# A graph layer's last stage: the sum of each row and its normed row made on GpSimd instead of ScalarE

## The chip, the cores and the metric

The kernel runs on one core of a Trainium2 chip. The metric is the device time of one execution in microseconds: the median over repeated runs of the kernel, without the profiler. The profile is of one further execution.

## The reference

A graph of 12,500 nodes with 256 channels and 212,500 weighted edges goes through one layer of four parts, all in float32:

```
xn = layernorm(x)
x  = x + segment_sum(w * (xn @ W)[dst], src) + mix(xn)   # linear attention, a small MLP, two layer norms
xh = layernorm(x)
s  = xh @ wr + br                      # one score for each row
sel = the 6249 rows with the highest scores
y  = (gelu(xh[sel] @ w1 + b1) @ w2 + b2) * s[sel]
out = x + xh;  out[sel] += y
```

What matters here is the last part. Every row needs its normed row `xh`, since the selected ones go through the feed-forward network, and the sum `x + xh`, which is the output of the rows that are not selected and the base to which the others add.

## The kernel before, in words

**Rows and tiles.** The 12,500 rows lie in 98 tiles of 128 rows. After the graph part and the mixing part, `x` of all rows stands in SBUF as `acc`, 98 tiles side by side, 256 float32 to a tile. The last stage handles them in 14 groups of G = 7 tiles; a group has 7 x 256 = 1792 columns.

**Up to the stage.** A loop sums sorted edge messages: VectorE builds weighted one-hots (L1822), TensorE multiplies, ScalarE evicts, and GpSimd adds 128x256 blocks into `acc` (L728). Then VectorE takes the statistics of every tile and the products with `wr` (L1841, L1843), ScalarE sums the products into the scores (L1348), and VectorE works out `rstd` and `minus` = -mean * rstd (L1861). Line 1862 makes `twice` = rstd + 1. The semaphore `norm_set` tells ScalarE that they are there.

**ScalarE's pass, `tail_rows` (L1352).** For a group n it writes, tile by tile, the normed rows `acc * rstd + minus` into one half of `rowbuf` (L1357, seven activations of 128x256), then the scores into a 257th column (L1359), and then, tile by tile, `acc * twice + minus` = x + xh into `x3[s]` (L1363, seven more). `rowbuf` has two halves and `x3` two buffers, `node` and a part of `tabs`; before a group writes one, it waits until the store of the group two before it has landed (`x3_out`, `base_out`). Each activation adds 1 to `rows_ready`, so 15 come from a group.

**SyncE's stores, `tail_store` (L594).** It waits for 8 of a group's 15 and stores the half of `rowbuf` to `sorted_rows` in HBM (L596, 903 KB), then waits for all 15 and stores `x3[s]` to the output (L605, 896 KB). All is in the order of the groups on one queue.

**VectorE meanwhile: the top-k.** From L1870 on it searches the score that 6249 rows reach, two bits a round in 16 rounds (L1881 to L1897). A round is a chain of small operations, each waiting for the one before: it forms three candidates (L1885, L1877 to L1879), compares the 98 scores of each partition with each (L1888, three times 128x98), counts (L1891), has TensorE sum the counts over the partitions (L1089), reads them from PSUM (L1894), and takes the bits over (L1895, L1897). Afterwards two prefix sums give each row its place (L1911 to L1918), and VectorE writes large one-hots over parts of `acc` that are no longer needed (L1949 to L1952, after the wait at L1948 for eight groups' `rows_ready`), then seven times L1957; TensorE turns them into the list of selected rows (L1105), and L1963 hands the first numbers to GpSimd.

**GpSimd meanwhile** has nothing to do: after L728 its next instruction is the first gather of selected rows, `x_fetch` (L741), which waits for the last stores and for `xid_ready` from L1963. From there to the end the feed-forward network runs over 25 blocks of 256 selected rows on TensorE (L1116 to L1135), with ScalarE, VectorE and GpSimd beside it.

Of the kernel before, what the change touches and what calls it, by code (L numbers as in the profile page):

```python
# [6 lines left out]
N, C, E, HEADS, HID, NQKV = 12500, 256, 212500, 8, 1024, 768  # L7
P = 128
# [35 lines left out]
G = 7  # L44
NG = NT // G
# [5 lines left out]
def gps_layer_kernel(nc, x, src, dst, edge_weight, gnn_w, wqkv, ln1_g, ln1_b, w1, b1, w2, b2,  # L51
# [3 lines left out]
    ALU, ACT, AX = mybir.AluOpType, mybir.ActivationFunctionType, mybir.AxisListType  # L55
    ds = bass.ds
# [14 lines left out]
    with ExitStack() as ctx:  # L71
        def sb(name, shape, dt=F32):
            return ctx.enter_context(nc.sbuf_tensor(name, shape, dt))

        def sem(name):
            return ctx.enter_context(nc.semaphore(name))


        acc = sb("acc", [P, NT * C])
# [22 lines left out]
        rowbuf = sb("rowbuf", [P, 2 * S, RW])  # L102
# [34 lines left out]
        def part(at, *shape, of=acc):  # L137
            n = int(np.prod(shape))
            ap = of[:, at:at + n]
            if len(shape) == 1:  # L140
                return ap
            if len(shape) == 2:
                return ap.rearrange("p (a b) -> p a b", a=shape[0])
            return ap.rearrange("p (a b c) -> p a b c", a=shape[0], b=shape[1])

        def half(at, n, of, dt=BF16):
            return of[:, at:at + n // 2].bitcast(dt)
# [6 lines left out]
        fw1_s = tabs[:, 0:CC * HID].rearrange("p (c h) -> p c h", c=CC)  # L154
        fw2_s = tabs[:, CC * HID:2 * CC * HID].rearrange("p (k c) -> p k c", c=C)
# [12 lines left out]
        GC = G * C  # L168
# [63 lines left out]
        wts, idx, place, rstd = (part(2560 + k * NT, NT, of=mb) for k in range(4))  # L232
# [6 lines left out]
        minus, twice, tile_b = part(4500, NT, of=mb), part(4600, NT, of=mb), half(4700, NT, mb)  # L239
# [9 lines left out]
        x3 = [node[:, 0:GC], tabs[:, 2 * CC * HID:2 * CC * HID + GC]]  # L249
# [50 lines left out]
        (qT_in, xnb_in, x_in, t_mm, x1_ready, x1T_mm, x1T_ready, h_mm, h_ready, y_mm, mix_done) = (sem(n) for n in (  # L300
            "qT_in", "xnb_in", "x_in", "t_mm", "x1_ready", "x1T_mm", "x1T_ready", "h_mm", "h_ready", "y_mm",
            "mix_done"))
        fw_in, w_in, w2_in, t_read, xnb_read, xb_ready, y_left = (sem(n) for n in (
            "fw_in", "w_in", "w2_in", "t_read", "xnb_read", "xb_ready", "y_left"))
        rows_left, norm_ready = sem("rows_left"), sem("norm_ready")
        passed, bits_ready = sem("passed"), sem("bits_ready")
        r_in = [sem(f"rows_in{k}") for k in range(KB)]
# [9 lines left out]
        base_out = [sem(f"base_out{s}") for s in range(2)]  # L317
# [63 lines left out]
        def _(sp):  # L381
# [205 lines left out]

            sp.wait_ge(perm_mm, NSB)
            sp.wait_ge(rhs_ready, NSB)
            sp.dma_start(fw1_s, fw1.rearrange("(k p) c -> p k c", p=P)).then_inc(fw_in, 16)  # L590
            sp.dma_start(fw2_s, fw2.rearrange("(k p) c -> p k c", p=P)).then_inc(fw_in, 16)


            def tail_store(g, s, last=False):  # L594
                sp.wait_ge(rows_ready, (2 * G + 1) * g + G + 1)
                sp.dma_start(lanes(tiles_of(rows_d[0:NT * P, :])[ds(G * g, G)]), rowbuf[:, s * G:(s + 1) * G, :]).then_inc(  # L596
                    x3_out[s], 16)
                sp.wait_ge(rows_ready, (2 * G + 1) * (g + 1))
                rows_ = x3[s].rearrange("p (t c) -> p t c", t=G)
                if last:  # L600
                    sp.dma_start(lanes(tiles_of(out[(NT - G) * P:(NT - 1) * P, :])), rows_[:, 0:G - 1, :]).then_inc(
                        base_out[s], 16)
                    sp.dma_start(out[(NT - 1) * P:N, :], rows_[0:LASTROWS, G - 1, :]).then_inc(base_out[s], 16)
                else:
                    sp.dma_start(lanes(tiles_of(out[0:(NT - 1) * P, :])[ds(G * g, G)]), rows_).then_inc(base_out[s], 16)  # L605

            with sp.Fori(0, NG // 2 - 1) as i:
                for s in range(2):
                    tail_store(2 * i + s, s)
            tail_store(NG - 2, 0)  # L610
            tail_store(NG - 1, 1, last=True)


        @block.gpsimd
        def _(pool):
            g = nc.gpsimd
# [19 lines left out]
            with pool.Fori(0, NG // 2) as i:  # L636
                chain.enter(i, 2 * G * 2)
                for n in range(2 * G):
                    s, t = n // G, n % G
# [90 lines left out]


            pool.sem_inc(fo_free, FO0)

            def x_fetch(i, s, after=True):

                pool.wait_ge(xid_ready, i + 1)
                if after:
                    pool.wait_ge(x3T_mm, i - 1)
                pool.sem_inc(passed, 1)
                for u in range(2):  # L740
                    g.indirect_dma_start(xc[s][:, u, :], None, rows_d[0:NT * P, :],  # L741
                                         bass.IndirectOffsetOnAxis(xid[:, s, u:u + 1], 0)).then_inc(xc_in[s], 16)
# [37 lines left out]
        def _(pe):  # L780
# [22 lines left out]
            for k, tab in enumerate((fbkt, floc, rew, fdrel)):  # L803
# [4 lines left out]
                for q in range(4):  # L808
                    n = min(4, T - 4 * q)
# [263 lines left out]
            with pe.Fori(0, steps) as i:  # L1073
                for k in range(KB):
                    pe.wait_ge(r_in[k], 16 * (i + 1))
                    pe.wait_ge(sums_ready, KB * i + k + 1)
                    for h in range(2):
                        grp = RG * i + 2 * k + h
                        for t in range(2):
                            pe.wait_ge(ohw_ready, 2 * grp + t + 1)  # L1080
                            s = 2 * h + t
# [19 lines left out]
            for q in range(G):  # L1101
                pe.wait_ge(cnt_ready, 18 + 3 + q)
                for t in range(LT):
                    i = LT * q + t
# [1 line left out]
                              start=i == 0, stop=i == NT - 1)  # L1106
                last.then_inc(cnt_mm, 1)

            pe.wait_ge(fw_in, 32)

            def served_transpose(i, s, turn):
                pe.wait_ge(xc_in[s], 32 * (turn + 1))
# [44 lines left out]
        def _(act):  # L1157
            A = nc.scalar.activation
# [13 lines left out]
            for job, o in enumerate(wq):  # L1172
                act.wait_ge(tab_mm, job + 1)
                if job == 4:
                    act.wait_ge(wraw_in, 112)
                    for c in range(CC):
                        last = A(o[:, c * C:(c + 1) * C], ps[:, job % 8, c * C:(c + 1) * C], ACT.Copy,
                                 scale=g1_c[:, c:c + 1])
# [5 lines left out]
            for k, outs in enumerate(tables):  # L1184
                for q in range(4):
                    job, n = 6 + 4 * k + q, min(4, T - 4 * q)
# [165 lines left out]
            def tail_rows(n, s, first=False):  # L1352

                if not first:
                    act.wait_ge(x3_out[s], 8 * (n - s))
                for t in range(G):
                    A(rowbuf[:, s * G + t, 0:C], acc[:, ds(n * GC + t * C, C)], ACT.Identity,  # L1357
                      scale=rstd[:, ds(G * n + t, 1)], bias=minus[:, ds(G * n + t, 1)]).then_inc(rows_ready, 1)
                A(rowbuf[:, s * G:(s + 1) * G, C], wts[:, ds(G * n, G)], ACT.Copy).then_inc(rows_ready, 1)  # L1359
                if not first:  # L1360
                    act.wait_ge(base_out[s], 8 * (n - s))
                for t in range(G):
                    A(x3[s][:, t * C:(t + 1) * C], acc[:, ds(n * GC + t * C, C)], ACT.Identity,  # L1363
                      scale=twice[:, ds(G * n + t, 1)], bias=minus[:, ds(G * n + t, 1)]).then_inc(rows_ready, 1)

            act.wait_ge(norm_set, 3)
            for s in range(2):
                tail_rows(s, s, first=True)
            with act.Fori(1, NG // 2) as i:
                for s in range(2):  # L1370
                    tail_rows(2 * i + s, s)
# [17 lines left out]
        def _(dve):  # L1389
            v = nc.vector  # L1390
# [222 lines left out]
            for q in range(4):  # L1613
                n = min(4, T - 4 * q)
# [221 lines left out]
            with dve.Fori(0, NG // 2) as i:  # L1836
                chain.enter(i, 2 * (2 * G + 1))
                for s in range(2):
                    n = 2 * i + s
# [19 lines left out]
            v_link(v.tensor_scalar(wts[:, :], wts[:, :], br_c[:, 0:1], None, ALU.add))  # L1859

            v.scalar_tensor_tensor(minus, mv[:, :, 0], -1.0, rstd[:, :], ALU.mult, ALU.mult).then_inc(norm_set, 1)  # L1861
            v.tensor_scalar(twice, rstd[:, :], 1.0, None, ALU.add).then_inc(norm_set, 1)
            v.sem_inc(norm_set, 1)
            chain.inc(v.tensor_copy(tile_b, cols[:, 0:NT]))
            chain.inc(v.memset(idl[:, 2 * FP:2 * FP + 4], 0))
# [79 lines left out]
            v_link(v.tensor_scalar(rI, pI, P - 1, None, ALU.bitwise_and))  # L1945
            chain.inc(v.tensor_copy(dv, dI))
            v_link(v.tensor_copy(md, rI))
            dve.wait_ge(rows_ready, (2 * G + 1) * 8)  # L1948
            v_link(v.tensor_tensor(spots, dv.unsqueeze(1).to_broadcast([P, 2 * FP, NT]),  # L1949
                                   cols[:, 0:2 * FP].unsqueeze(2).to_broadcast([P, 2 * FP, NT]), ALU.is_equal))  # L1950
            v.tensor_scalar(marks[:, 0, :, :], spots, lane[:, 0:1], None, ALU.mult).then_inc(cnt_ready, 1)
# [97 lines left out]
```

## Time and profile before

| | |
|---|---|
| median of 3 runs | 3774.55 us (3771.11 to 3775.57) |
| the profiled execution's own time | 3799.59 us |
| its span, first to last instruction | 3797.8 us |
| busy: TensorE matmul, VectorE, GpSimd, ScalarE | 3073.4, 2599.6, 2113.8, 1555.3 us |
| last stage before the feed-forward network | about 3296 to 3409 us of the span |
| feed-forward network | about 3415 us to the end |

The profile is one execution, with start and duration of every instruction on each engine, the semaphores that released it, and every DMA packet. PE is TensorE, PEld its weight loads, DVE VectorE, ACT ScalarE, POOL GpSimd, SPq the queue of SyncE on which the DMAs are issued. A duration is the time from the start of an instruction to its end, and holds whatever the instruction waited for in between.

### The profile page before, as it was taken

The numbers are of one execution on the slowest core, as the hardware profiler recorded it, in microseconds if no ns is written. First come the engines' busy times: TensorE is split into PE (matmuls) and PEld (weight loads), VectorE is DVE, ScalarE is ACT, GpSimd is POOL, SyncE is SP. The second block draws the span as 40 slices with busy tenths as digits, with TensorE's granted clock in tenths as the row PEclk, the third lists the DMA queues.
The fourth block names the chain that finished last, engine by engine and source line by source line (L and its number), as shares of the span: only waits on it lengthen the run. The fifth ranks groups of instructions, "written<-read, shape, count | busy, mean of one in ns | idle before, by whom it ended". The sixth has DMA issues, their size and how long they took to land.

```text
span 3797.8 us, 81728 instructions
## 1 busy us (share of the span) xinstructions
PE 3073.4 (81%) x18820; PEld 2305.1 (61%) x18820; DVE 2599.6 (68%) x6591; ACT 1555.3 (41%) x3781; POOL 2113.8 (56%) x2304
## 2 busy tenths in 40 slices
PE   3777738888888788888888886999999997029998
PEld 2444426666666666666676664777777775018887
DVE  6888884444444677777787773999999999861111
ACT  4444404555555444444444443333333333673222
POOL 1445534555555566666666565777777776003433
PEclk7899969999999999999899898999999999559999
DMA  5777727787777766666677666888888887161111
GB/s 162 239 262 261 256 73 239 263 261 254 252 264 262 237 229 217 216 215 222 222 228 231 203 211 221 272 278 276 277 276 277 277 277 229 62 217 50 54 52 44
DMA packets 427482, 818.33 MB, mean 215 GB/s; under 512 B 45499, under 2 KB 203191, under 8 KB 427256
## 3 DMA queue, kind: packets, MB, share of 16 engines
q1 hardware_dynamic: 348376, 559.80, 48.5%
q0 software_dynamic: 78880, 256.49, 17.7%
q14 instruction: 203, 1.66, 0.1%
q8 instruction: 23, 0.38, 0.0%
HBM read 459.96 MB, written 356.17 MB: 215 GB/s over the span
## 4 chain that ended last, share of the span: by engine, by line
PE 38%; issue 14%; DVE 14%; POOL 13%; ACT 6%; another core or an unknown queue 6%; DMA 3%; POOLq 3%; SPq 1%; DVEq 1%; ACTq 0%
POOL acc L728 13%; PE ps L948 12%; PE ps L1135 5%; PE ps L1125 5%; PE ps L961 3%; PE ps L995 2%; ACT rowbuf L1261 2%; POOLq L725 2%; PE ps L1082 2%; PE ps L1004 2%; DVE acc L1490 2%; PE ps L957 1%; DMA rowbuf<-sorted_rows 1%; DMA acc<-bucket_rows 1%
## 5 line engine op out<-in xcount | busy, mean ns | idle before, releaser
L695 POOL DMA_INDIRECT sorted_rows<-rowbuf,posu x896 | 1003.4, 1120 | 768.2 <-ACT rowbuf L1261 554.3
L948 PE MATMUL ps<-mainbuf 128*128 128x256 bf16 x5376 | 731.5, 280 | 195.7 <-ACT rowbuf L1261 140.5
L1082 PE MATMUL ps<-rowbuf,mainbuf 128*128 128x256 f32 x3584 | 844.7, 392 | 25.9 <-DVE mainbuf L1822 20.9
L1822 DVE TENSOR_SCALAR mainbuf<-cols,rowbuf 128x128 f32<-128x128 f32 x1792 | 820.9, 528 | 58.5 <-DMA rowbuf<-sorted_rows 50.2
L728 POOL TENSOR_TENSOR acc<-acc,node 128x256 f32 x896 | 673.3, 751 | 196.3 <-POOL acc L728 156.1
L1082 PEld LDWEIGHTS ps<-rowbuf,mainbuf 128*128 128x128 f32 x3584 | 620.3, 189 | 250.1 <-DVE mainbuf L1822 177.5
L948 PEld LDWEIGHTS ps<-mainbuf 128*128 128x128 bf16 x5376 | 502.2, 100 | 338.8 <-ACT rowbuf L1261 187.7
L1261 ACT ACTIVATE rowbuf<-ps 128x512 f32<-128x512 f32 x896 | 515.4, 594 | 447.2 <-PE ps L948 371.5
L1341 ACT ACTIVATE node<-ps 128x512 f32<-128x512 f32 x448 | 267.6, 597 | 603.0 <-PE ps L1082 499.4
L1665 DVE TENSOR_SCALAR mainbuf<-mainbuf,lane 128x1024 bf16<-128x1024 bf16 (+1 forms) x256 | 117.4, 458 | 254.4 <-PE ps L948 194.7
L1648 DVE TENSOR_TENSOR mainbuf<-tabs,cols 128x1664 bf16<-128x1664 f32 (+1 forms) x128 | 241.1, 1884 | 0.0
L1658 DVE TENSOR_REDUCE wl<-ps 128x14 f32<-128x28 f32 x128 | 24.1, 188 | 278.4 <-remote 245.0
L1331 ACT ACTIVATE rowbuf<-ps,fb_c 128x256 f32<-128x256 f32 x200 | 94.9, 474 | 253.7 <-PE ps L1125 245.2
L741 POOL DMA_INDIRECT acc<-sorted_rows,posu x50 | 48.6, 973 | 265.7 <-DVE posu L1963 197.3
L1252 ACT ACTIVATE wl<-ps 128x14 f32<-128x14 f32 x128 | 24.4, 190 | 407.8 <-DVE wl L1659 333.4
L961 PE MATMUL ps<-wqkvT,acc 128*128 128x512 f32 x392 | 185.5, 596 | 0.0
L852 PE MATMUL ps<-acc,mainbuf 128*128 128x416 f16 x512 | 125.4, 376 | 73.8 <-DVE acc L1490 73.8
L1135 PE MATMUL ps<-tabs,rowbuf 128*128 128x256 f32 x800 | 179.2, 382 | 5.4 <-ACT rowbuf L1331 5.1
L1125 PE MATMUL ps<-acc,tabs 128*128 128x256 f32 x800 | 179.3, 383 | 0.8 <-ACT acc L1326 0.8
L1135 PEld LDWEIGHTS ps<-tabs,rowbuf 128*128 128x128 f32 x800 | 149.9, 190 | 30.7 <-issue 9.6
L1651 DVE TENSOR_TENSOR mainbuf<-mainbuf,tabs 128x1092 bf16<-128x1092 bf16 x128 | 164.9, 1288 | 0.0
L1125 PEld LDWEIGHTS ps<-acc,tabs 128*128 128x128 f32 x800 | 146.0, 191 | 30.1 <-ACT acc L1326 1.2
(338 smaller groups left out, 4641.1 us busy)
## 6 DMA issues: line engine op xcount, KB each, us to landing
rowbuf<-sorted_rows SPq DMA_DIRECT2D x448, 516.0 KB, 4.5
mainbuf<-slot_rows_in_window SPq DMA_DIRECT2D x128, 448.0 KB
acc<-bucket_rows SPq DMA_DIRECT2D x128, 416.0 KB, 6.1
sorted_rows<-node SPq DMA_DIRECT2D x105, 258.0 KB, 2.4
mainbuf<-support_rows SPq DMA_DIRECT2D x128, 192.0 KB
sorted_rows<-rowbuf,posu POOLq DMA_INDIRECT x896
node<-in_x SPq DMA_DIRECT2D x104, 128.0 KB, 5.1
sorted_rows<-rowbuf SPq DMA_DIRECT2D x14, 903.0 KB, 4.9
```

The source lines that it names most:

```text
L695: g.indirect_dma_start(pairs_d, bass.IndirectOffsetOnAxis(posu[:, PC * k + c:PC * k + c + 1], 0), rowbuf[:, S * k + 2 * c:S * k + 2 * c + ...
L728: g.tensor_tensor(acc[:, ds(at, C)], acc[:, ds(at, C)], sums[:, k, h * C:(h + 1) * C], ALU.add).then_inc(acc_done, 1)
L948: last = mm(ps[:, MSG + (k + c) % 2, u * C:(u + 1) * C], oht[:, s * P:(s + 1) * P], win[:, k, v * C:(v + 1) * C], start=v == 0, stop=v == 2)
L961: last = mm(ps[:, KVPS + u, :], xnT_b[u][:, c * P:(c + 1) * P], wqkvT[:, c, C:3 * C], start=c == 0, stop=c == CC - 1)
L1082: last = mm(ps[:, GRP + k, h * C:(h + 1) * C], ohw[:, k % 2, s * P:(s + 1) * P], rowbuf[:, BT * k + s, 0:C], start=t == 0, stop=t == 1)
L1125: last = mm(ps[:, 2 + m % 2, 0:C], fw1_s[:, c, m * P:(m + 1) * P], x3T[:, s, c * 2 * P:(c + 1) * 2 * P], start=c == 0, stop=c == CC - 1)
L1135: last = mm(ps[:, 4 + s, u * C:(u + 1) * C], fhT[:, s, m, u * P:(u + 1) * P], fw2_s[:, m, :], start=m == 0, stop=m == HID // P - 1)
L1261: A(rowbuf[:, S * k + 2 * c:S * k + 2 * c + 2, 0:C], ps[:, MSG + (k + c) % 2, :].rearrange("p (t c) -> p t c", t=2), ACT.Copy).then_inc(ro ...
L1341: A(sums[:, k, :], ps[:, GRP + k, :], ACT.Copy).then_inc(sums_ready, 1)
L1648: v.tensor_tensor(ohp, pA[:, :, ds(i, 1)].to_broadcast([P, T, P]), cols[:, :].unsqueeze(1).to_broadcast([P, T, P]), ALU.is_equal).then_inc ...
L1651: v.tensor_tensor(rhs, ohs.unsqueeze(3).to_broadcast([P, T, S, V]), metab[:, ds(i, 1), :, :].rearrange("p a t v -> p (a t) v").unsqueeze(2 ...
L1822: v.tensor_scalar(ohw[:, k % 2, s * P:(s + 1) * P], cols[:, :], rowbuf[:, r, C + 1:C + 2], rowbuf[:, r, C:C + 1], ALU.is_equal, ALU.mult). ...
```

## The change

ScalarE writes only the normed rows and the scores: 8 increments of `rows_ready` from a group instead of 15. A new loop on GpSimd, `base_rows`, adds the seven normed tiles in `rowbuf` to the seven tiles of `acc` with one instruction of 128x1792 float32 and writes `x3[s]`; it waits for the group's 8 increments and, from the third group on, for the landing of the output store that last used `x3[s]`. Its semaphore `base_made` releases the output store, and ScalarE waits for it before it writes a half of `rowbuf` again. `twice` is gone. VectorE's wait before L1949 is now for eight `base_made`. To free a semaphore the loads of `fw1` and `fw2` count on `w_in` instead of `fw_in`; TensorE waits for the sum of both at the same place.

```diff
 sync:
-            sp.dma_start(fw1_s, fw1.rearrange("(k p) c -> p k c", p=P)).then_inc(fw_in, 16)
-            sp.dma_start(fw2_s, fw2.rearrange("(k p) c -> p k c", p=P)).then_inc(fw_in, 16)
+            sp.dma_start(fw1_s, fw1.rearrange("(k p) c -> p k c", p=P)).then_inc(w_in, 16)
+            sp.dma_start(fw2_s, fw2.rearrange("(k p) c -> p k c", p=P)).then_inc(w_in, 16)
             def tail_store(g, s, last=False):
-                sp.wait_ge(rows_ready, (2 * G + 1) * g + G + 1)
+                sp.wait_ge(rows_ready, (G + 1) * (g + 1))
...
-                sp.wait_ge(rows_ready, (2 * G + 1) * (g + 1))
+                sp.wait_ge(base_made, g + 1)
 gpsimd, between the loop of L728 and x_fetch:
+            def base_rows(n, s, first=False):
+                pool.wait_ge(rows_ready, (G + 1) * (n + 1))
+                if not first:
+                    pool.wait_ge(base_out[s], 8 * (n - s))
+                pool.sem_inc(passed, 1)
+                g.tensor_tensor(x3[s].rearrange("p (t c) -> p t c", t=G), rowbuf[:, s * G:(s + 1) * G, 0:C],
+                                acc[:, ds(n * GC, GC)].rearrange("p (t c) -> p t c", t=G),
+                                ALU.add).then_inc(base_made, 1)
+
+            for s in range(2):
+                base_rows(s, s, first=True)
+            with pool.Fori(1, NG // 2) as i:
+                for s in range(2):
+                    base_rows(2 * i + s, s)
 tensor:
-            pe.wait_ge(fw_in, 32)
+            pe.wait_ge(w_in, 16 * 6 + 32)
 scalar, tail_rows:
                 if not first:
                     act.wait_ge(x3_out[s], 8 * (n - s))
+                    act.wait_ge(base_made, n - 1)
...
-                if not first:
-                    act.wait_ge(base_out[s], 8 * (n - s))
-                for t in range(G):
-                    A(x3[s][:, t * C:(t + 1) * C], acc[:, ds(n * GC + t * C, C)], ACT.Identity,
-                      scale=twice[:, ds(G * n + t, 1)], bias=minus[:, ds(G * n + t, 1)]).then_inc(rows_ready, 1)
-            act.wait_ge(norm_set, 3)
+            act.wait_ge(norm_set, 2)
 vector:
-            v.tensor_scalar(twice, rstd[:, :], 1.0, None, ALU.add).then_inc(norm_set, 1)
...
-            dve.wait_ge(rows_ready, (2 * G + 1) * 8)
+            dve.wait_ge(base_made, 8)
```

On GpSimd, before, the end of the summing loop is followed at once by the gathers of `x_fetch` (`posu` is where the numbers of the selected rows lie):

```order
L728 TENSOR_TENSOR acc<-acc,node 128x256
L721 REGISTER_ALU
L721 COMPARE_AND_BRANCH
L741 DMA acc<-sorted_rows,posu 128x258 [waits base_out1,xid_ready,x3_out1,x3_out0,base_out0]
L741 DMA acc<-sorted_rows,posu 128x258
```

With the change, the adds of the 14 groups stand between them (lines after 733 are shifted by 15 or less in the changed file; its L756 is the gather):

```order
L728 TENSOR_TENSOR acc<-acc,node 128x256
L721 REGISTER_ALU
L721 COMPARE_AND_BRANCH
L739 TENSOR_TENSOR node<-rowbuf,acc 128x1792 [waits rows_ready]
L739 TENSOR_TENSOR tabs<-rowbuf,acc 128x1792 [waits rows_ready]
L745 UNCONDITIONAL_BRANCH
L745 ISA
L737 REGISTER_ALU [waits rows_ready]
L739 ISA [waits base_out0]
L739 TENSOR_TENSOR node<-rowbuf,acc 128x1792
```

Two stand ahead of a loop of six turns with two each. They were not there before; the gathers behind them are the same.

On SyncE, one turn of the store loop for the even group, before:

```order
L596 ISA [waits rows_ready]
L596 DMA sorted_rows<-rowbuf 128x7x258
L598 ISA
L605 ISA [waits rows_ready]
L605 DMA out_rows<-node 128x7x256
```

and with the change:

```order
L596 ISA [waits rows_ready]
L596 DMA sorted_rows<-rowbuf 128x7x258
L605 ISA [waits base_made]
L605 DMA out_rows<-node 128x7x256
```

The output store, and with it every store behind it on the queue, now waits for GpSimd instead of ScalarE.

## Rows read from the trace of the kernel before

**Rows 1.** The page's part 1: busy time, share of the span, instructions.
```profile
PE 3073.4 (81%) x18820; PEld 2305.1 (61%) x18820; DVE 2599.6 (68%) x6591; ACT 1555.3 (41%) x3781; POOL 2113.8 (56%) x2304
```

**Rows 2.** The chain that ended last, 3250 to 3800 us: start, us, what.
```profile
3390.75 3.44 ACT tabs L1363 x7
3394.18 21.82 issue
3416.08 0.61 ACT acc L1326
```

**Rows 3.** The waits, 3290 to 3430 us: us in total, times, longest.
```profile
POOL acc L741 <- DVE posu L1963: 197.3, 1, 197.3
```

**Rows 4.** Timeline, end of the stretch: start us, us, engine, line, op.
```profile
3378.03 5.26 DVE L1949 TENSOR_TENSOR acc<-mainbuf,cols 128x4900 bf16<-128x4900 f32 x1
...
3389.44 17.80 PE L1105 MATMUL ps<-acc,mainbuf 128*128 128x100 bf16 x98 [18.04 <-DVE mainbuf L1957]
...
3407.76 0.24 DVE L1963 COPY posu<-mainbuf 128x2 uint32<-128x2 uint32 x2
...
3408.96 0.98 POOL L741 DMA_INDIRECT acc<-sorted_rows,posu  x1 [197.34 <-DVE posu L1963]
```

**Rows 5.** Windows: length; busy PE, PEld, DVE, ACT, POOL; clock, DMA share, GB/s.
```profile
3301.30:3303.30 2.00, 0.00 (x0) 0.00 (x0) 0.95 (x7) 2.00 (x5) 0.00 (x0) 0.50 1.00 349
3304.90:3306.90 2.00, 0.00 (x0) 0.00 (x0) 0.97 (x6) 2.00 (x6) 0.00 (x0) 0.50 1.02 346
3300.00:3398.00 98.00, 12.33 (x69) 8.00 (x70) 69.92 (x266) 94.19 (x203) 0.00 (x0) 0.50 0.77 263
3398.60:3408.00 9.40, 8.64 (x48) 5.81 (x46) 5.33 (x8) 0.00 (x0) 0.00 (x0) 0.50 0.01 2
```

**Rows 6.** Timeline, start of the stretch, VectorE and ScalarE.
```profile
3296.19 0.20 DVE L1862 TENSOR_SCALAR mainbuf<-mainbuf 128x98 f32<-128x98 f32 x1
3296.31 0.20 DVE L1864 CAST mainbuf<-cols 128x98 bf16<-128x98 f32 x1
3296.43 3.55 ACT L1357 ACTIVATE rowbuf<-acc,mainbuf 128x256 f32<-128x256 f32 x7 [5.51 <-DVE mainbuf L1862]
...
3299.88 0.20 ACT L1359 ACTIVATE rowbuf<-mainbuf 128x7 f32<-128x7 f32 x1
3299.98 3.53 ACT L1363 ACTIVATE node<-acc,mainbuf 128x256 f32<-128x256 f32 x7
...
3303.42 3.53 ACT L1357 ACTIVATE rowbuf<-acc,mainbuf 128x256 f32<-128x256 f32 x7
```

**Rows 7.** DMA issues, 3290 to 3430 us: count, KB each, us to landing.
```profile
sorted_rows<-rowbuf SPq DMA_DIRECT2D x14, 903.0 KB, 4.9
out_rows<-node SPq DMA_DIRECT2D x7, 896.0 KB, 4.1
```

**Rows 8.** GpSimd's adds by line: count, ns min/median/max, first and last start.
```profile
L644 POOL TENSOR_TENSOR node<-node,rowbuf x49: 662/672/1017, 77.5 to 454.1; 128x256 f32<-128x256 f32 x49
...
L728 POOL TENSOR_TENSOR acc<-acc,node x896: 722/754/847, 2354.1 to 3210.9; 128x256 f32 x180
...
L705 POOL TENSOR_TENSOR node<-node,vec x49: 1268/1277/1289, 1293.8 to 2264.2; 128x512 f32<-128x512 f32 x49
```

**Rows 9.** Timeline around a long GpSimd operation, 499 to 507 us.
```profile
499.00 7.29 POOL L655 TENSOR_TENSOR tabs<-acc,tabs 128x1664 bf16<-128x1664 f32 x1
499.12 1.21 DVE L1468 TENSOR_TENSOR_SCAN mainbuf<-one,ps 128x512 f32<-128x512 f32 x1
...
500.36 5.47 DVE L1474 SCALAR_TENSOR_TENSOR small<-mainbuf 128x4 int32<-128x4 f32 x1
505.87 0.45 DVE L1475 TENSOR_SCALAR small<-small 128x4 int32<-128x4 int32 x1
```

**Rows 10.** VectorE operations by line: count, ns min/median/max.
```profile
L1490 DVE TENSOR_TENSOR acc<-acc,mainbuf x128: 1009/1019/7581, 73.3 to 528.5; 128x1664 f16<-128x1664 f16 x128
...
L1474 DVE SCALAR_TENSOR_TENSOR small<-mainbuf x32: 165/166/5470, 62.1 to 523.9; 128x4 int32<-128x4 f32 x32
...
L1822 DVE TENSOR_SCALAR mainbuf<-cols,rowbuf x1792: 332/346/907, 2348.9 to 3206.5; 128x128 f32<-128x128 f32 x200
...
L1508 DVE BATCH_NORM_STATS2 stats<-node x49: 401/408/428, 63.7 to 409.7; 128x6 f32<-128x256 f32 x49
```

**Rows 11.** Timeline, one of the sixteen top-k rounds.
```profile
3298.29 0.16 DVE L1885 TENSOR_TENSOR cands<-tk,mainbuf 128x3 int32<-128x3 int32 x1 [0.81 <-DVE tk L1874]
...
3299.09 0.63 DVE L1888 TENSOR_SCALAR mainbuf<-mainbuf,cands 128x98 f32<-128x98 f32 x3
3299.76 0.46 DVE L1891 TENSOR_REDUCE cntb<-mainbuf 128x3 bf16<-128x294 f32 x1
...
3300.50 0.16 DVE L1894 TENSOR_SCALAR cands<-ps 128x3 int32<-128x3 f32 x1 [0.28 <-PE ps L1089]
...
3301.01 0.55 DVE L1897 TENSOR_TENSOR tk<-tk,cands 128x1 int32<-128x1 int32 x3
3302.43 0.16 DVE L1885 TENSOR_TENSOR cands<-tk,mainbuf 128x3 int32<-128x3 int32 x1 [0.88 <-DVE tk L1897]
```

More of the change, by code:

```diff
@@ L302, in gps_layer_kernel @@
             "mix_done"))
-        fw_in, w_in, w2_in, t_read, xnb_read, xb_ready, y_left = (sem(n) for n in (
-            "fw_in", "w_in", "w2_in", "t_read", "xnb_read", "xb_ready", "y_left"))
+        base_made, w_in, w2_in, t_read, xnb_read, xb_ready, y_left = (sem(n) for n in (
+            "base_made", "w_in", "w2_in", "t_read", "xnb_read", "xb_ready", "y_left"))
         rows_left, norm_ready = sem("rows_left"), sem("norm_ready")
```

## The prediction

> **What bounds the kernel now.** Part 1 of the page [rows 1] gives TensorE the largest share of the span, but the change lies in one stretch of about 110 us in which TensorE is nearly idle, so the shares say nothing; that stretch has to be read alone. The chain of waits comes next [rows 2]. It names ScalarE's second pass L1363 as the last piece before the feed-forward network, and then 21.82 us of "issue", a stretch that nothing explains. So the chain is not to be trusted there: it fell back on ScalarE's own previous work. The wait list [rows 3] and the end of the timeline [rows 4] say what GpSimd's first gather L741, with which the network begins, waited for: it starts at 3408.96, 0.96 us after VectorE's L1963 is done, and L1963 hangs on TensorE's L1105 (done at 3407.2) and on VectorE's one-hots from L1949 on. The stores, which L741 needs as well, were ready long before: from 3398.6 to 3408.0 the DMA engines are busy for a share of 0.01 [rows 5]. **The bound of the stretch is VectorE's top-k chain**, 3296.3 to 3408.0; ScalarE's two passes and the stores end some 10 us earlier, beside it.
>
> **What is removed.** ScalarE loses 98 activations. By the timeline [rows 6] the first seven L1363 run from 3299.98 until the next group starts at 3303.42, so 3.44 us of each group and 14 x 3.44 = 48 us of ScalarE. All of it lies beside the top-k, with 10 us to spare: worth nothing. If that cover were gone, because VectorE were faster, the stores would bind next. On VectorE L1862 goes: the next instruction starts 0.12 us after it [rows 6], so -0.1 us on the path. The `fw` loads wait for the same things and are waited for at the same place: nothing.
>
> **How fast the new pipeline turns.** A group moves 903 + 896 KB [rows 7], which is 1.84 MB. In the two bursts of [rows 5] the DMA engines have a share of 1.00 and move 346 to 349 GB/s, so a group can't take less than 1.84 MB / 349 = 5.3 us. ScalarE needs 3.5 us for it [rows 6], and GpSimd some 4 us (below). ScalarE waits for the landing of the store two groups before; that takes 4.9 us alone, and more behind another store. So the stores pace the group, at 5.3 us: the last of 14 adds begins at about 3300 + 13 x 5.3 = 3369, and the last store has landed by about 3380. That is earlier than now and still not what L741 waits for.
>
> **What GpSimd's adds cost.** The trace has float32 adds of 256 columns with a median of 672 or 754 ns, and of 512 with 1277 ns [rows 8]. The second 256 columns cost 523 to 605 ns, so 1792 columns are 754 + 6 x 523 = 3.9 us or 672 + 6 x 605 = 4.3 us. I take 4.0 us. The bound above is seven times 754, 5.3 us, as if nothing were saved by one instruction. GpSimd is idle there today [rows 3], so none of this costs anything by itself: 14 x 4.0 = 56 us beside VectorE.
>
> **What the adds do to VectorE.** This is the term that decides. At 499.00 GpSimd begins a 7.29 us operation (L655), which ends at 506.29 [rows 9]. VectorE's L1474, on four columns, starts at 500.36 and takes 5.47 us; by its own row its minimum and median are 165 and 166 ns [rows 10]. L1475 behind it ends at 506.32, when GpSimd is through. The operations on SBUF operands behave alike over the trace: L1490, with two inputs, has a median of 1019 ns and a maximum of 7581; L1822, one input with factors from SBUF, has a minimum of 332 and a maximum of 907 ns in the loop in which L728 (754 ns) runs beside it. Other forms are not held up: L1468, with an input in PSUM, runs from 499.12 to 500.33 under the same L655, and the statistics L1508, with one input, stay between 401 and 428 ns. So a VectorE operation of the first kinds, issued during a GpSimd add, ends when the add ends. The Trainium skill says the same as a rule, in "SBUF — State Buffer", section "Who interferes with whom": the port pair that the two engines share is locked for a whole instruction, and a VectorE instruction with two SBUF inputs, or in a mode that uses both ports, "fully blocks" against GpSimd. By that rule the trace agrees, and a sum that leaves it out would be 46 us too short.
>
> Now one round of the top-k [rows 11]. It takes 4.14 us (3298.29 to 3302.43). L1885 to L1888 and L1895 to L1897 work on SBUF alone and are of the kinds that stop. From L1891 (one input, a reduction) over TensorE's sum to L1894 (from PSUM), 3299.76 to 3300.66, and in the gap of 0.88 us at the end of a round VectorE has nothing of the kinds that stop: 0.90 and 0.88 us in which an add costs nothing. So of an add of 4.0 us VectorE loses all but what it can still do before the next operation that stops: at most one such piece, say 0.9 us up to 1.05 with the waits at its ends, and at least nothing. The fixed part of the held-up instruction is also saved: L1475 took 0.45 us and ended 0.03 us after the add, where an operation of that size takes 0.17 (L1474), so 0.15 us. Recovered are 0.15 to 1.2 us of each add. I take the middle, 0.68, since an add starts where a store has landed, at any point of a round. **VectorE loses 14 x (4.0 - 0.68) = 46.5 us.** Ends: 14 x (3.9 - 1.2) = 38 us and 14 x (5.3 - 0.15) = 72 us.
>
> All 14 adds fall into the top-k: they end by 3373, and VectorE, held up, is then at about its seventh round of sixteen. So L1949's new wait for eight adds (the eighth is done by about 3341) is over long before VectorE comes there, and L1949 and L1957 meet no add. What follows L1949 is only moved: with it L741, and the network behind it.
>
> **Sum:** -0.1 + 46.5 = +46.4 us. Against its own execution: 3799.59 + 46.4 = 3846 us with the profiler. The median of the runs lies 25.0 us under the profiled execution; I take this for the same: 3774.55 + 46.4 = **3821 us**.
>
> **Rivals.**
> *Not slower: the two engines don't get into each other's way here.* The held-up instructions of [rows 9, 10] met GpSimd operations on other tiles; if what stopped them were an access to the same tile's memory, or if the adds with three plain float32 operands were free of it, VectorE would lose nothing, and 3774.4 us would result. Against it: L1822 reads `cols` and `rowbuf` and writes `mainbuf`, while L728 works on `acc` and `node`, as plain as the new add. It is no gain either, since the stores that end sooner aren't waited for. It decides below 0.5 us lost per add: 14 x 0.5 = 7 us, about what a measurement of this kernel can tell from no change (0.2%, 7.5 us). Chance 0.07; and 0.02 that something is faster for a reason I don't see, such as fewer wake-ups on the queues.
> *The add is far slower than the row of adds says.* At 5.3 us (seven single ones, or the address pattern of 7 pieces with a gap of 2 columns in `rowbuf`) it paces the pipeline instead of the DMA engines, above about 5.1 us with the 0.17 us between two. VectorE then gets nearly nothing between two adds: 14 x (5.3 - 0.68) = +65 us, 3839 us. L705 with 512 columns speaks against it. Chance 0.12.
> *Less is lost than I think, 20 to 38 us*, because the adds fall into the free pieces of a round by habit (VectorE runs free for a moment after each), or since only the read or only the write part of an add is exclusive: 3795 to 3812 us, say 3805. L1474 in [rows 9] ended 0.46 us before the add did, which speaks a little for it. Chance 0.14.
>
> **How the numbers follow.** Forecast, 38 to 55 us lost: 0.65. Range 3804 to 3842: it takes in the slow add (3839) and most of the third rival, and leaves out the 0.09 without a loss and the ends beyond. Slower 0.91, same 0.07, faster 0.02.
>
> **What would show it.** In the changed profile: GpSimd's new line with 14 instructions of 4.0 us; L1885 to L1897's counterparts with maxima of about 4 us and unchanged minima, while the reduction stays at 0.46 us; the top-k of 82 us long grown to about 128; ScalarE idle between groups, a period of 5.3 us on GpSimd and SyncE; GpSimd's first gather at 3408.96 + 46 = 3455, still released by VectorE; the network after it of the same length. Wrong would be: maxima of VectorE at their old values, or a first gather released by a store.

## The result, and the profile after

The changed kernel takes **3816.57 us** (median of 4 runs, 3807.39 to 3821.74) against 3772.98 us for the kernel before (4 runs): 43.6 us more, a ratio of 1.0109 with a 95% interval of 1.009 to 1.0129. Forecast were 3821 us, in a range of 3804 to 3842.

The two profiled executions can't be compared by their spans: that of before reached the stretch at 3296.43, that of after at 3266.69, though the work ahead of it is the same, and the profiled execution of before (3799.59 us) was 26.6 us above its median while that of after (3816.30 us) is at it. It is before's execution that is out of line: e2 and e7 below, built on the kernel before, reached the stretch at 3261.34 and 3265.32. So the comparison is made inside the stretch: from ScalarE's first normed row to GpSimd's first gather. Before that was 3296.43 to 3408.96, 112.53 us [rows 4, 6]. After, the timeline of the changed kernel shows (start us, us, engine, line, op):

```profile
3266.69 3.54 ACT L1373 ACTIVATE rowbuf<-acc,mainbuf 128x256 f32<-128x256 f32 x7 [5.39 <-DVE mainbuf L1872]
...
3394.76 5.26 DVE L1959 TENSOR_TENSOR acc<-mainbuf,cols 128x4900 bf16<-128x4900 f32 x1
...
3424.50 0.24 DVE L1973 COPY posu<-mainbuf 128x2 uint32<-128x2 uint32 x2
...
3425.69 0.97 POOL L756 DMA_INDIRECT acc<-sorted_rows,posu  x1 [81.19 <-DVE posu L1973]
```

That is 159.00 us, **46.5 us more**. From the start of L1959 (L1949 before) to the gather it is 30.93 us in both traces, and from the gather to the end 388.8 us in both. So all of it lies in VectorE's top-k, before L1959. The gather is still released by VectorE. GpSimd's new line, by its instructions (ns min/median/max):

```profile
L739 POOL TENSOR_TENSOR node<-rowbuf,acc x7: 3704/3711/3722, 3270.5 to 3335.5; 128x1792 f32<-128x1792 f32 x7
L739 POOL TENSOR_TENSOR tabs<-rowbuf,acc x7: 3616/3620/3647, 3274.2 to 3340.9; 128x1792 f32<-128x1792 f32 x7
```

and VectorE's operations in the sixteen rounds, the counterparts of L1877, L1879, L1888, L1891, L1894 and L1897:

```profile
L1887 DVE TENSOR_SCALAR cands<-cands x16: 168/169/3632, 3268.7 to 3376.6; 128x3 int32<-128x3 int32 x16
...
L1889 DVE TENSOR_TENSOR cands<-cands x16: 164/164/3597, 3269.2 to 3377.0; 128x3 int32<-128x3 int32 x16
...
L1898 DVE TENSOR_SCALAR mainbuf<-mainbuf,cands x48: 257/266/3673, 3269.3 to 3377.6; 128x98 f32<-128x98 f32 x48
...
L1901 DVE TENSOR_REDUCE cntb<-mainbuf x16: 461/461/462, 3270.0 to 3377.9; 128x3 bf16<-128x294 f32 x16
...
L1904 DVE TENSOR_SCALAR cands<-ps x16: 160/160/161, 3270.8 to 3378.6; 128x3 int32<-128x3 f32 x16
...
L1907 DVE TENSOR_TENSOR tk<-tk,cands x48: 158/159/3661, 3274.3 to 3379.5; 128x1 int32<-128x1 int32 x48
```

The minima and medians are those of before; a few instructions of every kind that works on SBUF alone took as long as an add. The operation that reads PSUM never did, though two of its sixteen began while an add ran. The reduction never did either, but here none began during an add, so this trace alone doesn't show that it would pass. The timeline of the changed kernel shows two adds and what they hit:

```profile
3292.13 0.16 DVE L1905 TENSOR_TENSOR cands<-cands,mainbuf 128x3 int32<-128x3 int32 x1
3292.18 3.70 POOL L739 TENSOR_TENSOR node<-rowbuf,acc 128x1792 f32<-128x1792 f32 x1 [2.43 <-ACT rowbuf L1375]
3292.32 3.97 DVE L1907 TENSOR_TENSOR tk<-tk,cands 128x1 int32<-128x1 int32 x3
...
3297.47 3.63 POOL L739 TENSOR_TENSOR tabs<-rowbuf,acc 128x1792 f32<-128x1792 f32 x1 [1.59 <-ACT rowbuf L1375]
3297.52 3.60 DVE L1888 TENSOR_SCALAR cands<-cands 128x3 int32<-128x3 int32 x1
```

The second add runs to 3301.10, and L1888, three integers in each partition, ends at 3301.12. From the second add on VectorE has, between two adds, only the gaps of 1.4 to 2.6 us in which GpSimd waits for ScalarE. Why ScalarE is late is told by the wait list (3290 to 3480 us: us in total, times, longest) and the windows (length; busy PE, PEld, DVE, ACT, POOL; clock, DMA share, GB/s):

```profile
ACT rowbuf L1373 <- DMA sorted_rows<-rowbuf: 15.9, 9, 2.1
...
3290.00:3340.00 50.00, 0.93 (x5) 0.52 (x5) 42.88 (x63) 34.14 (x76) 33.04 (x9) 0.50 1.03 339
3350.00:3420.00 70.00, 15.93 (x90) 10.75 (x90) 53.46 (x163) 0.00 (x0) 0.00 (x0) 0.50 0.00 0
```

The stores now fill the DMA engines (share 1.03, 339 GB/s, where it was 0.77 and 263 [rows 5]), ScalarE waits for their landing, and all of it is over some 75 us before anybody needs it.

### The profile page after: what moved, and what is told of

Same layout as the page of the kernel before. It is cut to its first block, busy times and chain, and to the rows that moved or that the text cites. A ratio compares the mean times of both kernels' runs of the same rounds, so it can differ in the third digit from the quotient of the medians.

```text
span 3814.5 us, 81616 instructions
## 1 busy us (share of the span) xinstructions
PE 3063.6 (80%) x18820; PEld 2303.1 (60%) x18820; DVE 2640.2 (69%) x6590; ACT 1510.4 (40%) x3683; POOL 2158.6 (57%) x2318
## 4 chain that ended last, share of the span: by engine, by line
PE 39%; POOL 15%; issue 14%; DVE 14%; ACT 5%; POOLq 4%; another core or an unknown queue 4%; DMA 2%; SPq 1%; DVEq 1%; ACTq 0%
POOL acc L728 15%; PE ps L963 12%; PE ps L1150 5%; PE ps L1140 5%; PE ps L976 3%; PE ps L1010 3%; POOLq L725 2%; PE ps L1019 2%; ACT rowbuf L1276 2%; PE ps L972 2%; DVE acc L1501 2%; DMA acc<-bucket_rows 1%; PE ps L1024 1%; PE ps L867 1%
## 5 line engine op out<-in xcount | busy, mean ns | idle before, releaser
L1833 DVE TENSOR_SCALAR mainbuf<-cols,rowbuf 128x128 f32<-128x128 f32 x1792 | 819.4, 526 | 57.2 <-DMA rowbuf<-sorted_rows 46.5
L728 POOL TENSOR_TENSOR acc<-acc,node 128x256 f32 x896 | 672.9, 751 | 195.9 <-POOL acc L728 145.4
```

Source lines behind the costliest of these rows:

```text
L728: g.tensor_tensor(acc[:, ds(at, C)], acc[:, ds(at, C)], sums[:, k, h * C:(h + 1) * C], ALU.add).then_inc(acc_done, 1)
L1833: v.tensor_scalar(ohw[:, k % 2, s * P:(s + 1) * P], cols[:, :], rowbuf[:, r, C + 1:C + 2], rowbuf[:, r, C:C + 1], ALU.is_equal, ALU.mult). ...
```

## The experiments

The theory: a GpSimd operation holds what VectorE's operations on SBUF need, for its whole length; the price is VectorE's lost time. The main rival: the new waits and the denser stores cost it. e1, e2, e6 and e7 ran on one chip, with the kernel before at 3773.81 us, and e3, e4, e5 and e8 on a chip on which the kernel before took 3616.92 us; each ratio is to the kernel before on the same chip. "Stretch" is measured in each profile as above.

| kernel | time, us | ratio to before (95%) | stretch, us | against 112.53 |
|---|---|---|---|---|
| changed kernel | 3816.57 | 1.009 to 1.0129 | 159.00 | +46.5 |
| e1 no add | 3772.12 | 0.9981 to 1.0002 | 112.43 | -0.1 |
| e2 spare adds in the kernel before | 3811.71 | 1.0086 to 1.0135 | 152.71 | +40.2 |
| e6 changed, operands in PSUM | 3777.91 | 0.9999 to 1.0018 | 119.15 | +6.6 |
| e7 before, operands in PSUM | 3778.40 | 1.0009 to 1.0029 | 115.29 | +2.8 |
| e3 two adds | 3705.32 | 1.0226 to 1.0267 | 199.14 | +86.6 |
| e4 fills in place of adds | 3643.57 | 1.0054 to 1.0099 | 132.28 | +19.8 |
| e5 seven small adds | 3651.15 | 1.0077 to 1.0111 | 143.69 | +31.2 |
| e8 busy TensorE in the kernel before | 3617.03 | 0.999 to 1.001 | 112.53 | 0.0 |

**e1: the pipeline without the add.**

```diff
-                g.tensor_tensor(x3[s].rearrange("p (t c) -> p t c", t=G), rowbuf[:, s * G:(s + 1) * G, 0:C],
-                                acc[:, ds(n * GC, GC)].rearrange("p (t c) -> p t c", t=G),
-                                ALU.add).then_inc(base_made, 1)
+                pool.sem_inc(base_made, 1)
```

> The changed kernel with every wait, store and semaphore of the new pipeline, but without the add itself: GpSimd only raises base_made, so the output of the rows that are not selected is left unmade. Port theory (VectorE is held up while a GpSimd add runs): nothing holds VectorE up, the stretch from ScalarE's first normed row to GpSimd's first gather is back at 112.5 us, and the time at 3773 us. Rival (the new waits, the order of the stores or the denser stores cost it): about 3816 us and a stretch of 159 us remain.

The stretch is 112.43 us, 0.10 us under before, and the time can't be told from the kernel before. The waits, the order and the density of the stores cost nothing: the DMA engines have a share of 1.04 and move 340 GB/s from 3290 to 3340 us of this run, as in the changed kernel. The 0.10 us is what L1862 was forecast to give (0.1).

**e2: the adds without the pipeline.**

```diff
             pool.sem_inc(fo_free, FO0)
+            pool.wait_ge(fw_in, 32)
+            for n in range(NG):
+                pool.wait_ge(rows_ready, (2 * G + 1) * n + G + 1)
+                pool.sem_inc(passed, 1)
+                g_link(g.tensor_tensor(wqkvT[:, :, :].rearrange("p c o -> p (c o)"), tabs[:, 0:CC * NQKV],
+                                       tabs[:, CC * HID:CC * HID + CC * NQKV], ALU.add))
```

> The kernel before, with 14 adds on GpSimd in the same stretch, one after each group's normed rows, of 1536 columns from tabs into wqkvT, tiles that VectorE does not touch there; nobody waits for them. By the slope of the adds one takes 3.2 us. Port theory: VectorE loses 14 x (3.2 - 0.34) = 40 us, 3813 us. Rivals: if the new waits cost it, or if VectorE is only held up by work on the same tile, 3773 us.

Stretch +40.2 us, 37.9 us slower in time. Nobody waits for these adds and they touch none of VectorE's tiles, so it is neither a new dependence nor a conflict over the same tile. The trace of this run shows one of its 14 adds and the operation that it stops:

```profile
3300.03 3.43 POOL L737 TENSOR_TENSOR wqkvT<-tabs 128x1536 f32<-128x1536 f32 x1 [3.55 <-ACT rowbuf L1365]
3300.11 0.16 DVE L1900 TENSOR_SCALAR cands<-ps 128x3 int32<-128x3 f32 x1 [0.28 <-PE ps L1095]
3300.41 3.06 DVE L1901 TENSOR_TENSOR cands<-cands,mainbuf 128x3 int32<-128x3 int32 x1
```

An add took 3.42 us, not 3.2; it began in a free piece of the round, let L1900 (from PSUM) pass, and stopped L1901. So did all 14. 40.2 / 14 = 2.87 us for an add, so 0.55 us of each were recovered, where 0.34 were expected: that the total came out as expected (40) is two errors that cancel.

**e6 and e7: the same top-k with one operand of each operation in PSUM**, in the changed kernel and in the kernel before.

```diff
-            wm, pen = scr[:, 0:NT], scr[:, NT:2 * NT]
+            in_ps = ps[:, 7, 0:12].rearrange("p (a k) -> p a k", k=3).bitcast(I32)
+            wm, pen = ps[:, 7, 128:128 + NT], scr[:, NT:2 * NT]
...
-            key, taken = tki[:, 0:1], tki[:, 1:2]
+            key, taken = ps[:, 7, 16:17].bitcast(I32), ps[:, 7, 17:18].bitcast(I32)
...
-                v_link(v.tensor_tensor(candi[:, 0, :], key.to_broadcast([P, 3]), pair, ALU.bitwise_or))
-                decode(candi[:, 0, :], candi[:, 1, :], candi[:, 2, :])
+                v_link(v.tensor_tensor(in_ps[:, 0, :], key.to_broadcast([P, 3]), pair, ALU.bitwise_or))
+                decode(in_ps[:, 0, :], in_ps[:, 1, :], candi[:, 1, :], candi[:, 2, :])
...
```

> The changed kernel with one operand of every top-k operation in PSUM instead of SBUF (the key, two of the candidates, the masked scores), so that none has two inputs in SBUF and none reads and writes SBUF alone. Port theory: the sixteen rounds take 66 us as before although the adds run beside them; only the prefix sums meet the last two adds, which costs 7 to 12 us: 3780 to 3785 us. If it is the time of GpSimd's work or the waits and not the operands' place, about 3816 us remain.

> The kernel before with the same operands in PSUM, as the control of the run above: what the move to PSUM costs or gives by itself. All theories: within 3 us of the kernel before, 3770 to 3776 us; the stretch 110 to 115 us.

The GpSimd adds are all there and as long as before, and the sixteen rounds don't notice them: from the start of the first reduction (L1902 in e6) to the end of the last they take 64.24 us with the adds (e6) and 64.32 without (e7), where the changed kernel takes 108.33 and the kernel before 61.85. In the rounds of e6 141 operations of VectorE began while an add ran, nine reductions, which still go from SBUF to SBUF, among them, and none took more than 0.02 us over its minimum. A round of e6 beside an add:

```profile
3299.78 3.71 POOL L739 TENSOR_TENSOR node<-rowbuf,acc 128x1792 f32<-128x1792 f32 x1 [1.94 <-ACT rowbuf L1375]
3299.88 0.17 DVE L1896 TENSOR_TENSOR ps<-ps,mainbuf 128x3 int32<-128x3 int32 x1 [0.82 <-DVE ps L1908]
...
3300.48 0.16 DVE L1890 TENSOR_TENSOR cands<-ps,cands 128x3 int32<-128x3 int32 x1
3300.68 0.77 DVE L1899 TENSOR_SCALAR mainbuf<-ps,cands 128x98 f32<-128x98 f32 x3
3301.49 0.46 DVE L1902 TENSOR_REDUCE cntb<-mainbuf 128x3 bf16<-128x294 f32 x1
```

The last two adds reach the prefix sums, whose operands stayed in SBUF, and each stops one operation there. The first of them makes the copy L1923 0.75 us long instead of 0.21, the second is shown. Together that is the 3.9 us between e6 and e7; 7 to 12 had been expected, so e6 came in below its 3780 to 3785 us:

```profile
3337.70 3.62 POOL L739 TENSOR_TENSOR tabs<-rowbuf,acc 128x1792 f32<-128x1792 f32 x1 [1.22 <-ACT rowbuf L1375]
...
3337.77 3.66 DVE L1926 TENSOR_TENSOR mainbuf<-mainbuf 128x94 f32<-128x94 f32 x1
```

(The first line is of GpSimd, the second of VectorE.) The move costs 2.8 us by itself (mostly the three comparisons, 0.77 instead of 0.63 us in a round); e7 lies just above what was expected of it, in time (3770 to 3776) and in the stretch (110 to 115). So e6 beats the changed kernel by 39 us and the kernel before not at all.

**e3: a second add for each group**, of 1536 columns, behind the first; the loop is written out, and GpSimd first waits for the weights to have landed.

```diff
+                g_link(g.tensor_tensor(wqkvT[:, :, :].rearrange("p c o -> p (c o)"), tabs[:, 0:CC * NQKV],
+                                       tabs[:, CC * HID:CC * HID + CC * NQKV], ALU.add))
...
```

> The changed kernel with a second add of 1536 columns on GpSimd (from tabs into wqkvT, needed by nobody) behind each of the 14. One of 1792 columns took 3.66 us, so one of 1536 takes 3.2 us; GpSimd then paces a group at about 7 us and the adds last 100 us. Port theory: 28 adds are paid one by one, 46.5 + 40 = 86 us over the kernel before, stretch 199 us, 3860 us. Rival (the pace of stores and waits costs it): little over 3816 us, since the stores get slower by no more than the adds' pace.

+86.6 us of stretch, 88.4 us in time. The price grows with the adds' total: 28 adds, 99.2 us of GpSimd, 86.6 us of VectorE. 28 operations were stopped, one for each add.

**e4: GpSimd only writes.** This kernel leaves out the sums for the output rows. Its loop is written out as in e3.

```diff
-                g.tensor_tensor(x3[s].rearrange("p (t c) -> p t c", t=G), rowbuf[:, s * G:(s + 1) * G, 0:C],
-                                acc[:, ds(n * GC, GC)].rearrange("p (t c) -> p t c", t=G),
-                                ALU.add).then_inc(base_made, 1)
+                g.memset(x3[s], 0.0).then_inc(base_made, 1)
+                g_link(g.memset(wqkvT[:, :, :].rearrange("p c o -> p (c o)"), 0.0))
...
```

> The changed kernel with the add replaced by two fills (1792 columns of x3, 1536 of wqkvT; some 3 us together), so the sums of the output rows are left out: GpSimd then writes SBUF as long as nearly the add did, but reads nothing. If the hold-up is of both a read and a write side, VectorE's two-input operations (whose one output does not need the second write side) pass, while the one-input operations on SBUF alone still stop: 10 to 30 us over the kernel before. If any GpSimd operation stops all of them: 14 x (3.0 - 0.34) = 37 us. If only GpSimd's reads matter: nothing, stretch 112.5 us.

+19.8 us, inside the 10 to 30 that a hold-up by kind of operation was to give. The two fills of a group took 3.0 us together. The operations of this run, in the order of a round (L1892 and L1885 are the counterparts of L1885 and L1878 before; L1895 of L1888; L1902 and L1904 of L1895 and L1897):

```profile
L1892 DVE TENSOR_TENSOR cands<-tk,mainbuf x16: 161/163/164, 3118.0 to 3199.2; 128x3 int32<-128x3 int32 x16
...
L1885 DVE TENSOR_SCALAR cands<-cands x16: 169/1304/1304, 3118.4 to 3199.6; 128x3 int32<-128x3 int32 x16
...
L1895 DVE TENSOR_SCALAR mainbuf<-mainbuf,cands x48: 264/266/1768, 3118.8 to 3200.3; 128x98 f32<-128x98 f32 x48
...
L1902 DVE TENSOR_TENSOR cands<-cands,mainbuf x16: 161/163/165, 3120.6 to 3201.7; 128x3 int32<-128x3 int32 x16
...
L1904 DVE TENSOR_TENSOR tk<-tk,cands x48: 158/159/161, 3120.8 to 3202.3; 128x1 int32<-128x1 int32 x48
```

26 two-input operations began while a fill ran, twelve each of L1892 and L1904 and two of L1902, and none took over 0.165 us. Of the operations from SBUF to SBUF with one input L1884, L1885 and L1895 began during a fill 26 times, and every time they took longer than their minimum, up to 1.68 us. Beside an add, which reads as well, both kinds were. That is the distinction of the Trainium skill, "SBUF — State Buffer", section "Who interferes with whom": two SBUF inputs contend only with a GpSimd instruction that reads SBUF, a two-port mode with any. In which mode the one-input operations ran no trace here shows.

**e5: seven adds of 256 columns in place of one of 1792**, the same sums.

```diff
-                g.tensor_tensor(x3[s].rearrange("p (t c) -> p t c", t=G), rowbuf[:, s * G:(s + 1) * G, 0:C],
-                                acc[:, ds(n * GC, GC)].rearrange("p (t c) -> p t c", t=G),
-                                ALU.add).then_inc(base_made, 1)
+                for t in range(G):
+                    add = g.tensor_tensor(x3[s][:, t * C:(t + 1) * C], rowbuf[:, s * G + t, 0:C],
+                                          acc[:, ds(n * GC + t * C, C)], ALU.add)
+                    add.then_inc(base_made if t == G - 1 else passed, 1)
```

> The changed kernel with seven adds of 256 columns for each group in place of one of 1792: the same sums. Seven take 5.1 us with 0.17 us between them, 6.2 us a group, so GpSimd is the pace, and the adds last 87 us. Port theory: VectorE gets one or two operations in each gap, as L1822 did beside L728, so it goes at about half its speed beside them: 40 to 55 us over the kernel before, 3813 to 3828 us. If each add had a fixed price on VectorE, 98 of them would cost far more than 14: over 3850 us.

+31.2 us of stretch and 34.2 us in time, less than the 40 to 55 expected, and 15 us less than with the long adds, though GpSimd's adds are busy for 66.9 us instead of 51.3. Where the expectation failed: I had taken the time of L728 (0.75 us, 0.17 us between two) for them. In this trace an add has a median of 0.64 to 0.72 us, and the adds of a group follow each other without gaps worth naming:

```profile
L740 POOL TENSOR_TENSOR node<-rowbuf,acc x49: 630/721/792, 3124.3 to 3194.3; 128x256 f32<-128x256 f32 x49
L740 POOL TENSOR_TENSOR tabs<-rowbuf,acc x49: 632/644/739, 3128.9 to 3199.9; 128x256 f32<-128x256 f32 x49
...
3162.66 4.46 POOL L740 TENSOR_TENSOR tabs<-rowbuf,acc 128x256 f32<-128x256 f32 x7 [0.91 <-ACT rowbuf L1376]
```

(The last row is of the timeline.) So they end as early as the long ones (80.0 us into the stretch against 77.8), and VectorE gets an operation in at the end of each. What is recovered of one add is (66.9 - 31.2) / 98 = 0.36 us, nearly the 0.34 of a long one (below); only there are seven times as many. Eight of the sixteen reductions (L1902 here) began during an add and none took over 0.464 us, which is what the changed kernel's trace could not show.

**e8: is it the clock that makes what follows the top-k long?** TensorE gets 328 matmuls of zeros in its idle time, 14 behind each count, 24 and 80 behind the two sums after the rounds.

```diff
+            def turn_over(n):
+                for _ in range(n):
+                    mm(ps[:, 5, 0:208], zeros_b[:, 0:P], zeros_b[:, :], start=True, stop=True)
...
```

> The kernel before, with matmuls of zeros (128x208, into a PSUM bank that nobody reads) on TensorE in its idle time during the top-k, where its granted clock is 0.50. It asks what the low clock costs, since the other runs leave L1105 (17.8 us for 98 matmuls at clock 0.50) as the largest piece behind the top-k. If the clock is granted in full then, L1105 is paced by VectorE's one-hots at 2.0 to 2.5 us each, 14 to 16 us, and the first turn of the network loses 2.4 us: 3 to 6 us faster, 3768 us. If the clock stays at 0.50: no change, or slower where a burst delays a count.

No change: 3617.03 against 3616.92 us, and the stretch is 112.53 us to the hundredth. By the windows of this run the granted clock was full (1.00) only from about 3182.3 to 3185.5 and from 3192.5 to 3199.1 us, behind the added matmuls, and was back at 0.50 when the matmuls for the list of rows came, which took 17.80 us as before (columns as above):

```profile
3175.00:3195.00 20.00, 15.32 (x111) 12.88 (x110) 16.35 (x71) 20.00 (x44) 0.00 (x0) 0.65 0.77 260
3195.00:3205.00 10.00, 1.81 (x22) 1.57 (x19) 9.96 (x5) 10.00 (x22) 0.00 (x0) 0.71 0.79 270
3205.00:3224.00 19.00, 17.80 (x98) 12.17 (x98) 12.73 (x11) 4.77 (x11) 0.00 (x0) 0.50 0.36 121
```

What a full clock there would give is left open.

## Why the prediction was right

**The bound.** VectorE's chain, not ScalarE's, was the bound, as read from the wait list against the chain of waits. e1 has ScalarE's second pass gone and nothing else added, and gains 0.1 us: the pass was worth nothing.

**The pace.** 5.3 us a group was forecast from 1.84 MB at 349 GB/s. From the fourth add on they start 5.0 to 6.1 us apart, the last at 3340.85, 74.2 us into the stretch; 3369 against 3296.4, 73 us, was forecast.

**The price of an add.** 4.0 us was taken, of 3.9 to 4.3; measured were 3.62 and 3.71 us (two medians, by the tile written), below the lower end. The slope from 256 to 512 columns (523 ns) was a little too steep: from one tile of 0.64 us in e5 to seven in 3.62 it is 0.50 us a tile.

**What VectorE loses.** Each add was to cost its length less 0.68 us, the middle of 0.15 and 1.2. It costs its length less 0.34: 51.3 / 14 = 3.66 us of add, 46.5 / 14 = 3.32 us of loss. So the two terms of the product were both off, by +0.34 and by -0.34, and the sum of 46.5 us came out to the tenth by their cancelling. As a forecast of the mechanism it is confirmed; as a forecast of the number it was lucky. The step that was mis-sized is that the middle of the two ends was taken for the mean. An add that starts at any point of a round mostly meets VectorE among operations that stop: by the starts of the operations in the sixteen rounds before, the next that stops is 0.38 us away on average, and with its own 0.16 us that makes an estimate of 0.54 us, not 0.68. And the starts were not spread evenly. Three of the fourteen adds began in a free piece and 0.59 to 0.72 us were recovered; the other eleven began among operations that stop, for 0.15 to 0.35 us. In the changed kernel fourteen operations between L1887 and L1907 lasted over half a microsecond more than their minimum, as many as there are adds. In e2, where all the adds began in a free piece, 0.55 us were recovered: the habit that the third rival spoke of is there, with a smaller effect.

**The rivals.** "They don't get into each other's way" is refuted by e1 and e2 together; a conflict over a tile by e2 alone. "The add is far slower" is refuted by its row. "Less is lost, since only the read or only the write part is exclusive" is half true as a mechanism (e4) and false for an add, which does both.

**The medians** differ by 43.6 us where the stretch grew by 46.5; the interval of the ratio, 34 to 49 us, holds both.

## What to carry to other kernels

An engine that is idle is not free if its operations stop those of the engine that bounds the stretch, as GpSimd's adds stopped VectorE's here: price an operation moved to GpSimd by what VectorE loses, 0.84 to 0.91 of its length for these long adds (e2, e3, the changed kernel), before asking what it takes off ScalarE. Being tiny doesn't spare a VectorE operation: one of 0.16 us was stopped for the whole of an add. If the GpSimd work has to lie there, short instructions cost less than long ones (31 against 46 us), and an operand of VectorE's in PSUM takes the conflict away nearly altogether (6.6, of which 2.8 are the move's own price).

## What the runs showed that I had not expected

An operation on three integers, 0.16 us long, waits for 3.6 us, and ends only 0.02 us after the add does. Adds of 256 columns in a row ran without the 0.17 us between them that L728 has, which also loads a register for its address each time. And the stretch was the same to a hundredth of a microsecond in two executions whose kernel times lie 5% apart (112.53 us in before, at 3799.59, and in e8, at 3614.91 us), while the kernel's time varies by some 10 us: a change confined to a stretch is read more sharply there than in the total.
